# Experts' tiles written out, q and k parts in halves, maxima spread by ScalarE, last sums in PSUM

## The chip, the core and the metric

The kernel runs on one core of one Trainium2 chip. The metric is the device time of one execution in microseconds (us): the median of three runs. Below, PE is TensorE, DVE is VectorE, ACT is ScalarE, POOL is GpSimd, and SP is SyncE, which here only starts transfers.

## The reference

Two layers on x of 16 batches of 256 rows of 128 numbers. Layer 0 is attention with a mask in 16 heads of 64, and then 16 experts of which each row uses four. Layer 1 is attention in 16 heads of 8, and then a recurrence over the batches. Each of the four parts is added to x and normalized. The last two, which most of the change touches:

```python
q = _split_heads(_lora_linear(x, Wq, Aq, Bq), b, n)   # k and v likewise
attn = jnp.einsum('bhnd,bhmd->bhnm', q, k) * SCALE
attn = jax.nn.softmax(attn, axis=-1)
out = jnp.einsum('bhnm,bhmd->bhnd', attn, v)
...
def step(c, xt):
    ft = jax.nn.sigmoid(xt @ wf.T + c @ uf.T + bf)
    it = jax.nn.sigmoid(xt @ wi.T + c @ ui.T + bi)
    gt = jnp.tanh(xt @ wc.T + c @ uc.T + bc)
    c = ft * c + it * gt
    return (c, None)
c_final, _ = lax.scan(step, c0, x)
h = jnp.tanh(jnp.einsum('tbi,oi->tbo', x, wo) + c_final @ uo.T + bo)
```

Every output needs the state after the last batch, so the final tanh of all batches comes behind the whole scan.

## The kernel before

The program has one stream of instructions on each engine, tied together by semaphores. The stages follow one another: attention of layer 0; experts; a hand-over; attention of layer 1 together with the recurrence; a last stage.

*Experts.* 4096 rows by four experts are sorted into 144 tiles of 128 rows, written to memory (xs), and gathered by tile. `tiles` computes TURN = 24 tiles: transposed rows (xgT), eight products with the first weights (line 869), gelu on ACT, eight with the second weights (878). `batch_loop` (line 42) writes two turns out, then runs a hardware loop over the turns between, then writes one out. With six turns the loop body runs three times, so each engine jumps back twice: between tiles 71 and 72, and between tiles 95 and 96.

*Hand-over.* POOL gathers each batch's expert rows (yk, line 615, four gathers in a half, two halves a batch), ACT weighs them with the gates (1146), POOL combines them (641 to 645). The deviation and norm of a batch go from DVE to POOL (rstd, a power, 623) and back. The order on POOL is `outputs(b)`: deviations, new state, first half of a fetch, keep, combine, second half.

*Layer 1.* A batch takes eight steps p of two heads each. PE makes each product of q and k twice: `scores` gives the row maxima for the next batch, and line 897 gives the transposed scores of this batch with the maxima subtracted (the maxima are three more rows of the stacked operand qst). ACT takes exponentials (1096), PE multiplies with v (909). q and k are split in three bfloat16 parts (`parts`, on ACT and DVE), stored to memory (qkd) and loaded back stacked (qst, kst) for the batch after next. SP starts all of that in order: the spread of the second half of the maxima for this batch (TMB), two stores, nine loads and one fill with zeros for the batch after next, the spread of the first half of the next batch's maxima (TMA, line 460). Line 897 waits for the first half at p = 0 and for the second at p = 4, and at each p for the exponentials of the step before. The scores of p = 0 wait for all loads of the next batch (`stk`). At p = 4 and 6 PE makes the gates of the recurrence for batch b - 2 (988, 989, 992), ACT applies sigmoid and tanh, POOL makes the new state c2 (651 to 657).

*Last stage.* After the last state PE makes the product with uo (999), DVE adds the bias to it (1480, tile `state`) and adds that to three of four groups of four batches (1484), POOL adds it to the fourth (678). ACT takes tanh of each group (1161), DVE (1491) and POOL (682) add x, the last norm follows (DVE, POOL, ACT 1166), and SP stores each group.

## Time and profile before

| what | us |
|---|---|
| median of three runs | 1545.09 (1543.08 to 1546.7) |
| profiled execution, its own time | 1541.06 |
| its span | 1539.3 |
| experts, roughly | 709 to 1001 of the span |
| hand-over | 1001 to 1079 |
| batches of layer 1 | 1079 to 1464 |
| last stage | 1464 to 1539.3 |

The prediction is for the median; rows of the trace belong to the profiled execution. Over the span PE is busy 1277.0 us (83%), DVE 1012.2, ACT 943.3 and POOL 795.4. Such shares hide that the stages differ, so the views are read by stretch.

### The profile page before, as it was taken

To read this page: it belongs to the slowest core of one execution; us is meant where nothing else is said; L and a number is where in the kernel's file an instruction comes from. 1 tells how busy PE (TensorE), PEld (TensorE's weight loads), DVE (VectorE), ACT (ScalarE), POOL (GpSimd) and SP (SyncE) were. 2 spreads that over 40 slices of the span, in tenths; PEclk is the share of its full clock that TensorE was granted. 3 is DMA by queue.
4 is the path that set the end of the run, shared out by engine and by line. 5 is a ranking of instruction groups with operands and counts; after the bars stand their busy time and mean duration, and the time that the engine had idled before them with its cause. 6 is when DMAs were issued, how large, how long until landed. Compare 5 with 4: busy or idle time off the path is not lost.

```text
span 1539.3 us, 36468 instructions
## 1 busy us (share of the span) xinstructions
PE 1277.0 (83%) x9486; PEld 963.4 (63%) x9486; DVE 1012.2 (66%) x3750; ACT 943.3 (61%) x2844; POOL 795.4 (52%) x1025
## 2 busy tenths in 40 slices
PE   7999999999999999856999899903778777787870
PEld 3766666766666666636999889901445555555540
DVE  1677777777777777755777666615677677667725
ACT  5877777777777777733566556511555566555544
POOL 1557777777777777743332100166456665653133
PEclk9999999999999999977999999955899989999995
DMA  9522222222222222111222222215343434343201
GB/s 345 168 61 68 68 66 66 68 68 68 68 68 68 68 68 68 44 45 51 71 70 70 61 62 69 63 34 100 80 88 69 89 66 92 72 87 58 47 4 55
DMA packets 150447, 115.49 MB, mean 75 GB/s; under 512 B 11809, under 2 KB 139937, under 8 KB 148290
## 3 DMA queue, kind: packets, MB, share of 16 engines
q1 hardware_dynamic: 142146, 97.50, 24.7%
q0 software_dynamic: 8192, 16.79, 4.0%
q8 instruction: 38, 0.62, 0.2%
q14 instruction: 71, 0.58, 0.1%
HBM read 50.02 MB, written 61.08 MB: 72 GB/s over the span
## 4 chain that ended last, share of the span: by engine, by line
PE 28%; DMA 7%; issue 5%; DVE 5%; DVEq 3%; POOL 2%; ACT 2%; another core or an unknown queue 2%; SPq 1%; POOLq 1%; ACTq 0%
PE psum L869 9%; PE psum L878 8%; DMA qst<-mrow 3%; PE psum L909 3%; DMA wall<-mrow 3%; PE psum L897 2%; PE psum L972 2%; POOL yk L615 1%; PE psum L855 1%; PE psum L988 1%; ACT wall L1096 1%; DVE mx L1396 1%; PE psum L989 1%; DMA yk<-ys,posc 1%
## 5 line engine op out<-in xcount | busy, mean ns | idle before, releaser
L526 POOL TENSOR_SCALAR P<-P,rinv 128x192 f32<-128x192 f32 (+1 forms) x384 | 308.5, 817 | 163.9 <-DVE rinv L1223 161.2
L1056 ACT ACTIVATE P<-shifted,least 128x192 f32<-128x192 f32 (+1 forms) x512 | 240.3, 471 | 113.0 <-DVE least L1209 112.3
L1086 ACT ACTIVATE hid<-psum,wA 128x128 f32<-128x128 f32 x576 | 164.4, 368 | 118.3 <-PE psum L869 118.2
L1396 DVE TENSOR_REDUCE mx<-psum 128x2 f32<-128x512 f32 x256 | 165.6, 687 | 78.4 <-PE psum L972 54.1
L1096 ACT ACTIVATE wall<-psum 128x1024 f32<-128x1024 f32 x128 | 130.9, 1022 | 93.8 <-PE psum L897 73.7
L1209 DVE CUSTOM_DVE_ANT_0 shifted<-psum,band 128x192 f32<-128x192 f32 (+1 forms) x512 | 168.7, 384 | 27.6 <-PE psum L747 27.3
L869 PE MATMUL psum<-xgT,wA 128*128 128x128 f32 x1152 | 156.7, 280 | 7.6 <-DVE xgT L1362 7.6
L516 POOL DMA_INDIRECT xs<-x1c,pos x128 | 127.9, 999 | 57.9 <-issue 29.6
L615 POOL DMA_INDIRECT yk<-ys,posc x128 | 124.7, 974 | 55.7 <-issue 29.3
L878 PE MATMUL psum<-wB,hid 128*128 128x128 f32 x1152 | 153.3, 277 | 0.0
L869 PEld LDWEIGHTS psum<-xgT,wA 128*128 128x128 f32 x1152 | 144.1, 197 | 8.3 <-issue 8.3
L878 PEld LDWEIGHTS psum<-wB,hid 128*128 128x128 f32 x1152 | 141.5, 194 | 0.0
L783 PEld LDWEIGHTS psum<-ident,P 128*128 128x128 f32 x1024 | 117.5, 141 | 36.3 <-issue 29.3
L783 PE MATMUL psum<-ident,P 128*128 128x128 f32 x1024 | 134.9, 275 | 3.6 <-POOL P L526 1.4
L747 PE MATMUL psum<-kT,qT 64*128 64x192 f32 (+1 forms) x1024 | 131.5, 375 | 0.6 <-DVE least L1209 0.6
L801 PE MATMUL psum<-PT,V 128*64 128x256 f32 (+1 forms) x1024 | 111.0, 359 | 0.7 <-DVE PT L1197 0.7
L747 PEld LDWEIGHTS psum<-kT,qT 64*128 64x128 f32 x1024 | 80.2, 186 | 38.6 <-issue 37.4
L1355 DVE COPY wA<-wall 128x516 f32 x144 | 61.9, 430 | 60.6 <-ACT hid L1086 39.8
L1056 ACT ACTIVATION_READ_ACCUMULATOR P<-shifted,least 128x1 f32 x512 | 95.8, 187 | 0.0
L698 PE MATMUL psum<-hT,wg 128*128 (+1 forms) x256 | 88.9, 429 | 1.8 <-ACT kT L1013 0.9
L1197 DVE COPY PT<-psum 128x448 f32<-128x448 f32 x128 | 79.0, 617 | 17.3 <-PE psum L801 8.5
L801 PEld LDWEIGHTS psum<-PT,V 128*64 128x64 f32 x1024 | 67.9, 136 | 30.2 <-issue 8.1
(243 smaller groups left out, 2547.5 us busy)
## 6 DMA issues: line engine op xcount, KB each, us to landing
xs<-zrow SPq DMA_DIRECT2D x33, 1024.0 KB
xg<-xs SPq DMA_DIRECT2D x144, 64.0 KB, 1.8
ys<-yrow SPq DMA_DIRECT2D x72, 128.0 KB, 1.8
wall<-in_wall SPq DMA_DIRECT2D x1, 8232.0 KB, 35.9
qkd<-parts SPq DMA_DIRECT2D x32, 192.0 KB
qst<-qkd SPq DMA_DIRECT2D x66, 64.0 KB
wall<-qkd SPq DMA_DIRECT2D x35, 64.0 KB
kst<-qkd SPq DMA_DIRECT2D x11, 192.0 KB
```

Of the source, the lines that this page charges most:

```text
L526: g.tensor_scalar(x, x, rinv[:, par, n:n + 1], None, ALU.mult).then_inc(s["pn_ready"], 1)
L615: g.indirect_dma_start(out=yk[:, slot, count * half + n, :], out_offset=None, in_=ys, in_offset=bass.IndirectOffsetOnAxis(posc[:, half, n: ...
L747: last = mm(bk[:, c0:c0 + w], qT[64 * h:64 * h + 64, p, it * 128:(it + 1) * 128], kT[64 * h:64 * h + 64, p, 0:w], start=True, stop=True)
L783: last = nc.tensor.transpose(bk[:, c0:c0 + 128], P[:, par1, it, h, jt * 128:(jt + 1) * 128], ident[:, :])
L801: last = mm(OTB[64 * h:64 * h + 64, k * N + c0:k * N + N], V[:, jt, r * 128 + 64 * h:r * 128 + 64 * h + 64], PT[:, k, h, keys], start=(jt ...
L869: mm(UP[two][:, at:at + GT], wA[:, p % 4, f * 128:(f + 1) * 128], xgT[:, p % 4, :], start=True, stop=True).then_inc(s["up_mm"], 1)
L878: last = mm(DN[two][:, 0:D], hid[:, m, f, :], wB[:, m, f * D:(f + 1) * D], start=(f == 0), stop=(f == FC - 1))
L1056: last = sc.activation(P[:, par, it, h, 0:w], shifted[:, par, it, h, 0:w], ACT.Exp, scale=-1.0, bias=least[:, par, n:n + 1], accum_out=row ...
L1086: sc.activation(hid[:, p % 4, f, :], UP[two][:, at:at + GT], ACT.Gelu, bias=wA[:, p % 4, F + f:F + f + 1]).then_inc(s["hid_ready"], 1)
L1096: sc.activation(pc[:, p % 4, :, :, :].rearrange("q h j n -> q (h j n)"), ST, ACT.Exp, scale=SCALE1).then_inc(s["exps1"], 1)
L1209: v.tensor_tensor_reduce(out=shifted[:, par, it, h, 0:w], in0=bk[:, c0:c0 + w], in1=band[:, it, 0:w], scale=-SCALE0, scalar=3.0e38, op0=AL ...
L1396: v.tensor_reduce(out=mx[:, :, h], in_=SB[(par + 1 + h) % 3].rearrange("q (i n) -> q i n", i=TT), axis=mybir.AxisListType.X, op=ALU.max).t ...
```

## The change

1. All 144 experts' tiles are written out on SP, PE, ACT and DVE; no loop is left there (TURN is 8, which sets only how many one call writes).
2. qkd holds q and k by halves of the heads. Four stores of 64 partitions take the place of two of 128; each load is as large as before, in twice as many pieces of half the size. The matrix cwqk is put in the same order, in four DVE operations for two.
3. The maxima are spread by a transfer that ACT starts right after its own copy, no longer by SP.
4. In step 7 PE makes the scores ahead of the transposes of x2 and x3.
5. POOL's first gathers are interleaved with combine and deviations, and ACT weighs the rows of two early batches at another place.
6. POOL adds the bias bo2 to each batch's output xo; the last two states are made on DVE.
7. In the last stage the sums are made in PSUM: PE brings the outputs in with the identity (`outputs_in`, eight matmuls of 128x512) and adds the state's product (`state_in`, sixteen matmuls of 256 columns). ACT's tanh reads PSUM. The tile `state`, DVE's lines 1480 and 1484 and POOL's 678 and 682 go. Of the last group ACT scales half and DVE half, and it is stored in two parts.

```diff
-TURN = 24
+TURN = 8
...
-        qkd = nc.dram_tensor("qkd", (2, NPART, 128, N), bf16, kind="Internal").ap()
+        qkd = nc.dram_tensor("qkd", (2, 2, NPART, 64, N), bf16, kind="Internal").ap()
...
-            batch_loop(sp, 2, NT // TURN - 1, 2, body)
+            for i in range(NT // TURN + 1):
+                body(i)
...
             def attention(b, par):
-                if has(b, 0):
-                    spread_maxima(b, TMB, par, 1)
                 if has(b, 2):
                     load = (par + 2) % 3
                     need_alone(sp, "parts_ready", b + 3)
                     need_alone(sp, "stk", 16 * NSTK * (b + 2))
                     for w in range(2):
-                        sp.dma_start(qkd[w].rearrange("a r n -> r a n"), parts[:, :, w * N:(w + 1) * N]).then_inc(s["qkd_out"], 16)
-                    need_alone(sp, "qkd_out", 32 * (b + 3))
+                        for e in range(2):
+                            sp.dma_start(qkd[w, e].rearrange("a r n -> r a n"), parts[64 * e:64 * e + 64, :, w * N:(w + 1) * N]).then_inc(s["qkd_out"], 16)
+                    need_alone(sp, "qkd_out", 64 * (b + 3))
                     need_alone(sp, "st_full", 8 * b)
-                    rows = qkd.rearrange("w a (d h) n -> w (a d) h n", h=H1)
+                    rows = [qkd[w].rearrange("e a (d h) n -> (a d) e (h n)", h=H1 // 2) for w in range(2)]
+                    q, k = [x[load].rearrange("q (e h) n -> q e (h n)", e=2) for x in (qst, kst)]
                     n = 0
                     for qa in range(NPART):
                         count = NPART - qa
-                        sp.dma_start(kst[load][DH1 * n:DH1 * (n + count), :, :], rows[1, 0:DH1 * count, :, :]).then_inc(s["stk"], 16)
-                        for k in range(count):
-                            sp.dma_start(qst[load][DH1 * (n + k):DH1 * (n + k + 1), :, :], rows[0, DH1 * qa:DH1 * (qa + 1), :, :]).then_inc(s["stk"], 16)
+                        sp.dma_start(k[DH1 * n:DH1 * (n + count), :, :], rows[1][0:DH1 * count, :, :]).then_inc(s["stk"], 16)
+                        for m in range(count):
+                            sp.dma_start(q[DH1 * (n + m):DH1 * (n + m + 1), :, :], rows[0][DH1 * qa:DH1 * (qa + 1), :, :]).then_inc(s["stk"], 16)
                         n += count
-                    sp.dma_start(qst[load][MROW:MROW + NMAX, :, :], no_maxima).then_inc(s["stk"], 16)
-                if has(b, 1):
-                    spread_maxima(b, TMA, (par + 1) % 3, 0)
...
+            sp.wait_ge(s["fin_ready"], GROUPS)
+            store(8 * GROUPS - 8, 4)
+            sp.wait_ge(s["fin_dve"], 1)
+            store(8 * GROUPS - 4, 4)
...
+                if has(b, -2):
+                    need_alone(pool, f"free{GB[0]}", tally[GB[0]].before(b, GB[1] + 1))
+                    xo = xo_all[:, bass.ds((b - 2) * TT, TT), :]
+                    g.tensor_tensor(xo, xo, bo2[:, :].rearrange("q (o d) -> q o d", o=1).to_broadcast([128, TT, D]), ALU.add).then_inc(s["xo_kept"], 1)
...
-            for b in range(-5, 2):
+            fetch(-5, -5 % 3, 0)
+            fetch(-5, -5 % 3, 1)
+            fetch(-4, -4 % 3, 0, 0, 2)
+            combine(-4, -4 % 3)
+            fetch(-4, -4 % 3, 0, 2, 3)
+            deviations(-3)
+            fetch(-4, -4 % 3, 0, 3, 4)
+            fetch(-4, -4 % 3, 1)
+            keep(-3)
+            fetch(-3, -3 % 3, 0)
+            combine(-3, -3 % 3)
+            fetch(-3, -3 % 3, 1, 0, 1)
+            deviations(-2)
+            fetch(-3, -3 % 3, 1, 1, 4)
+            keep(-2)
+            fetch(-2, -2 % 3, 0)
+            combine(-2, -2 % 3)
+            fetch(-2, -2 % 3, 1)
+            for b in range(-1, 2):
...
-            xo, xt = group(GROUPS - 1)
-            pool.wait_ge(s["state_ready"], 1)
-            g.tensor_tensor(xo, xo, per_batch(state), ALU.add).then_inc(s["h_pre_last"], 1)
.then_inc(s["last_sum"], 1)
...
+                        if isinstance(b, int) and b == B + 1:
+                            last_gates(b)
+                        else:
+                            need(pe, "scan_done", b - 1)
+                            need_x2T_x3T(pe, b)
+                            gates(b, GA)
+                    if p == 5 and isinstance(b, int) and b == B:
+                        outputs_in(0)
+                        outputs_in(1)
...
+                    scores(b, p, nxt)
                     if p == 7 and (has(b, 3) or has(b, -1)):
...
-                    scores(b, p, nxt)
...
+            def last_gates(b):
+                need_x2T_x3T(pe, b)
+                parts = (GA, 0, 0), (GA, 1, 1), (GB, 0, 2)
+                for use, n, k in parts:
+                    need_free(pe, b, use)
+                    mm(shared(use)[:, n * N:(n + 1) * N], gw[:, k, :], x3T[:, :], start=(n == 0), stop=False)
+                for it in range(TT):
+                    mm(shared(GB)[:, N + it * D:N + (it + 1) * D], x3T[:, it * 128:(it + 1) * 128], gw[:, 3, :], start=False, stop=False)
+                outputs_in(2)
+                need(pe, "scan_done", b - 1)
+                for use, n, k in parts:
+                    last = mm(shared(use)[:, n * N:(n + 1) * N], gu[:, k, :], c2[:, :], start=False, stop=(n == 1 or use == GB))
+                    if n == 1 or use == GB:
+                        last.then_inc(s[f"full{use[0]}"], 1)
+            def outputs_in(c):
+                need(pe, "xo_kept", 4 * (c + 1))
...
+                for half in range(2):
+                    mm(bank[2 * c + half][:, :], ident[:, :], xo_all[:, 8 * c + 4 * half:8 * c + 4 * half + 4, :].rearrange("q t d -> q (t d)"), start=True, stop=False)
+            def state_in(c):
+                wo3 = gu[:, 3, :].rearrange("q (o d) -> q o d", o=1).to_broadcast([128, 2, D])
+                for half in range(2):
+                    for it in range(TT):
+                        last = mm(bank[2 * c + half].rearrange("q (k i d) -> q k i d", k=2, i=TT)[:, :, it, :], c2[:, it * 128:(it + 1) * 128], wo3, start=False, stop=(it == TT - 1))
+                last.then_inc(s["h_full"], 1)
             attention_loop(pe, attention)
             pe.wait_ge(s["scan_done"], B + 1)
-            for it in range(TT):
-                last = mm(SB[0][:, it * D:(it + 1) * D], c2[:, it * 128:(it + 1) * 128], gu[:, 3, :], start=True, stop=True)
-            last.then_inc(s["state_mm"], 1)
+            state_in(0)
+            state_in(1)
+            outputs_in(3)
+            state_in(2)
+            state_in(3)
...
+                    if p == 1 and isinstance(b, int) and b in (-2, -1):
+                        for half in range(2):
+                            weigh(b - 1, (b - 1) % 3, half)
...
-            def maxima_row(b, use, half):
+            def maxima_row(b, use, slot, half):
                 need_full(act, b, use)
                 sc.activation(mrow[:, half, :], shared(use).bitcast(bf16)[0:NMAX, 0:N], ACT.Copy).then_inc(s[f"free{use[0]}"], 1)
+                need_alone(act, f"free{use[0]}", tally[use[0]].before(b, use[1] + 1))
+                hh = H1 // 2
+                act.dma_start(qst[slot][MROW:MROW + NMAX, half * hh:half * hh + hh, :],
+                              mrow[:, half, :].rearrange("q (o n) -> q o n", o=1).to_broadcast([NMAX, hh, N])).then_inc(s["mrow_in"], 16)
...
+                act.wait_ge(s["h_full"], c + 1)
+                sc.activation(xo_all[:, 8 * c:8 * c + 8, :].rearrange("q t d -> q (t d)"), psum[:, 1024 * c:1024 * c + 1024], ACT.Tanh).then_inc(s["h_act"], 1)
...
+                    if p == 7 and isinstance(b, int) and b >= B:
+                        dve.wait_ge(s["gate_act"], b - 1)
+                        v.scalar_tensor_tensor(tf[:, :], tf[:, :], 1.0, c2[:, :], ALU.add, ALU.mult)
+                        v.scalar_tensor_tensor(tg[:, :], ti[:, :], 1.0, tg[:, :], ALU.add, ALU.mult)
+                        v.drain()
+                        v.scalar_tensor_tensor(c2[:, :], tf[:, :], 0.5, tg[:, :], ALU.mult, ALU.add).then_inc(s["scan_done"], 1)
...
-            dve.wait_ge(s["state_mm"], 1)
-            need(dve, f"free{GB[0]}", tally[GB[0]].before(B + 2))
-            v.tensor_tensor(state[:, :, :], SB[0][:, 0:N].rearrange("q (i d) -> q i d", i=TT), bo2[:, :].rearrange("q (o d) -> q o d", o=1).to_broadcast([128, TT, D]), ALU.add)
-            v.drain().then_inc(s["state_ready"], 1)
-            for c in range(GROUPS - 1):
-                xo, xt = group(c)
-                v.tensor_tensor(xo, xo, per_batch(state), ALU.add).then_inc(s["h_pre"], 1)
             def squared(c):
                 x, h = x_all[:, 8 * c:8 * c + 8, :], xo_all[:, 8 * c:8 * c + 8, :]
+                dve.wait_ge(s["h_act"], c + 1)
+                v.tensor_tensor(x, x, h, ALU.add)
...
+                if c == GROUPS - 1:
+                    for k in range(4, 8):
+                        x = x_all[:, 8 * c + k, :]
+                        last = v.tensor_scalar(x, x, mv2[:, c, k, 0:1], rstd2[:, c, k:k + 1], ALU.subtract, ALU.mult)
+                    last.then_inc(s["fin_dve"], 1)
```

SP in a batch of layer 1, before: the stores of the parts, the loads for the batch after next (tile wall is one of three that hold qst and kst), then the spread of the maxima.

```order
L440 DMA qkd<-parts 128x3x256 x2
L448 DMA wall<-qkd 24x4096
L450 DMA wall<-qkd 8x4096 x3
L448 DMA wall<-qkd 16x4096
L450 DMA wall<-qkd 8x4096 x2
L448 DMA wall<-qkd 8x4096
L450 DMA wall<-qkd 8x4096
L452 DMA wall<-zeros 24x4096
L460 DMA qst<-mrow 24x8x256 x2
```

The same place now.

```order
L432 DMA qkd<-parts 64x3x256 x4
L441 DMA wall<-qkd 24x2x2048
L443 DMA wall<-qkd 8x2x2048 x3
L441 DMA wall<-qkd 16x2x2048
L443 DMA wall<-qkd 8x2x2048 x2
L441 DMA wall<-qkd 8x2x2048
L443 DMA wall<-qkd 8x2x2048
L445 DMA wall<-zeros 24x2x2048
L432 DMA qkd<-parts 64x3x256 x4
```

The last row before is gone from SP; the stores are four, the pieces 2x2048 for 4096.

ACT in a batch before: an exponential, the copy of the maxima, weighing of gathered rows, exponentials and copies between.

```order
L1096 ACTIVATE wall<-psum 128x1024
L1151 ACTIVATE mrow<-psum 24x256
L1146 ACTIVATE yk<-yk,gcur 128x128 x4
L1096 ACTIVATE wall<-psum 128x1024
L1100 ACTIVATE oTc<-psum 128x256
L1146 ACTIVATE yk<-yk,gcur 128x128 x4
L1096 ACTIVATE wall<-psum 128x1024
```

The same place now.

```order
L1155 ACTIVATE wall<-psum 128x1024
L1211 ACTIVATE mrow<-psum 24x256
L1214 DMA qst<-mrow 24x8x256
L1205 ACTIVATE yk<-yk,gcur 128x128 x4
L1155 ACTIVATE wall<-psum 128x1024
L1159 ACTIVATE oTc<-psum 128x256
L1205 ACTIVATE yk<-yk,gcur 128x128 x4
L1155 ACTIVATE wall<-psum 128x1024
```

The spread of the maxima stands between ACT's copy and its next work.

PE at the program's end, before: the last gates, then the product of state and uo.

```order
L989 MATMUL psum<-c,gu 128x256
L988 MATMUL psum<-x3T,gw 128x256
L989 MATMUL psum<-c,gu 128x256
L992 MATMUL psum<-gw,x3T 128x128 x2
L999 MATMUL psum<-gu,c 128x128 x2
```

The same place now: products of x3T, outputs (wall, with the identity), then those that need the state c.

```order
L1017 MATMUL psum<-x3T,gw 128x256 x3
L1019 MATMUL psum<-gw,x3T 128x128 x2
L1041 MATMUL psum<-wall,ident 128x512 x2
L1023 MATMUL psum<-c,gu 128x256 x3
L1048 MATMUL psum<-gu,c 128x2x128 x8
L1041 MATMUL psum<-wall,ident 128x512 x2
L1048 MATMUL psum<-gu,c 128x2x128 x8
```

What doesn't need the last state moved ahead of it, and the sums of the groups came in.

## Rows read from the trace of the kernel before

**Rows 1.** Busy time by stretch: length, busy us per engine, granted clock, DMA share, GB/s.

```profile
756.00:804.00 48.00, 48.00 (x433) 48.00 (x432) 35.59 (x103) 28.55 (x101) 16.05 (x27) 1.00 0.25 72
1001.00:1079.00 78.00, 16.02 (x53) 7.48 (x54) 24.75 (x63) 13.98 (x41) 50.44 (x66) 0.52 0.33 67
1079.00:1464.00 385.00, 305.78 (x2544) 203.40 (x2544) 276.72 (x822) 223.81 (x441) 198.79 (x268) 0.93 0.38 74
1464.00:1539.30 75.30, 27.11 (x194) 18.54 (x192) 33.23 (x143) 33.62 (x68) 26.89 (x29) 0.71 0.11 30
```

**Rows 2.** Timeline of PE over a back edge: start, duration, instruction, idle and releaser.

```profile
850.81 1.07 PE L869 MATMUL psum<-xgT,wA 128*128 128x128 f32 x8
...
856.75 2.01 PE L869 MATMUL psum<-xgT,wA 128*128 128x128 f32 x8 [3.87 <-DVE xgT L1362]
...
860.38 1.06 PE L869 MATMUL psum<-xgT,wA 128*128 128x128 f32 x8
```

**Rows 3.** Waits over the second back edge: total us, times, longest us.

```profile
DVE wA L1355 <- issue: 4.3, 3, 3.4
...
PE psum L869 <- DVE xgT L1362: 3.8, 1, 3.8
```

**Rows 4.** Timeline of the hand-over.

```profile
1029.24 0.16 DVE L94 TENSOR_TENSOR u<-rstd 128x2 f32<-128x2 f32 x1 [5.25 <-POOL rstd L623]
...
1054.67 1.28 ACT L1146 ACTIVATE yk<-yk,gcur 128x128 f32<-128x128 f32 x4 [16.77 <-DMA yk<-ys,posc]
...
1066.23 0.37 ACT L1151 ACTIVATE mrow<-psum 24x256 bf16<-24x256 bf16 x1 [3.71 <-issue]
...
1078.95 1.03 PE L897 MATMUL psum<-qst,kst 128*128 128x256 bf16 x4 [6.86 <-DMA qst<-mrow]
```

**Rows 5.** Chain that ended last: start, duration, step.

```profile
1044.32 10.33 DMA yk<-ys,posc
...
1069.37 9.54 DMA qst<-mrow
...
1087.65 2.43 DMA qkd<-parts
...
1531.81 3.85 ACT x_all L1166 x10
```

**Rows 6.** Line 460, the spread of the maxima: its issues, and who waited for it.

```profile
L460 SPq DMA_DIRECT2D qst<-mrow x22: 778/818/1583, 1069.4 to 1468.2; - x22
...
  PE psum L897: 34.9, 11
```

**Rows 7.** Timeline of three places in the batches of layer 1.

```profile
1101.03 1.02 ACT L1096 ACTIVATE wall<-psum 128x1024 f32<-128x1024 f32 x1 [1.35 <-remote]
...
1102.64 1.03 PE L897 MATMUL psum<-qst,kst 128*128 128x256 bf16 x4 [2.97 <-DMA qst<-mrow]
...
1103.60 1.94 PE L909 MATMUL psum<-wall,v 128*32 128x256 f32 x16
...
1387.03 0.60 PE L897 MATMUL psum<-wall 128*128 128x256 bf16 x4
...
1387.99 1.07 PE L909 MATMUL psum<-wall,v 128*32 128x256 f32 x16 [0.36 <-DVEq L1462]
...
1438.98 1.02 ACT L1096 ACTIVATE wall<-psum 128x1024 f32<-128x1024 f32 x1
...
1444.16 1.04 PE L897 MATMUL psum<-wall 128*128 128x256 bf16 x4 [4.34 <-DMA wall<-mrow]
```

**Rows 8.** Waits in the batches: total us, times, longest us.

```profile
POOL rstd L623 <- DVE ve L89: 108.3, 16, 16.4
```

**Rows 9.** Timeline after the last gates.

```profile
1500.38 0.40 POOL L651 TENSOR_SCALAR tf<-tf 128x256 f32<-128x256 f32 x1 [6.15 <-ACT tg L1122]
...
1504.07 1.22 PE L999 MATMUL psum<-gu,c 128*128 128x128 f32 x4 [4.39 <-POOL c L657]
1505.32 0.42 DVE L1480 TENSOR_TENSOR state<-psum,bo 128x256 f32<-128x256 f32 x1 [15.18 <-PE psum L999]
...
1509.31 4.27 ACT L1161 ACTIVATE wall<-wall 128x1024 f32<-128x1024 f32 x4 [8.85 <-DVE wall L1484]
1511.47 1.21 DVE L1491 TENSOR_TENSOR x_all<-x_all,wall 128x1024 f32<-128x1024 f32 x1
```

**Rows 10.** Groups by line: instructions, busy us, mean ns, idle before.

```profile
L705 PE MATMUL psum<-wg,hV 128*128 128x512 f32 x128 | 66.6, 602 | 3.3 <-issue 1.7 <-DVE V L1184 0.8 <-DVE rconst L1179 0.4
...
L615 POOL DMA_INDIRECT yk<-ys,posc x128 | 124.7, 974 | 55.7 <-issue 29.3 <-POOL posc L612 26.4
```

More of the change, by code:

```diff
@@ L647, in new_state @@
             def new_state(b):
-                if has(b, -2):
+                if has(b, -2) and not (isinstance(b, int) and b >= B):
                     need_alone(pool, "gate_act", b - 1)
@@ L879, in tiles @@
                         last.then_inc(s["dn_mm"], 1)
-            batch_loop(pe, 2, NT // TURN - 1, 2, tiles)
+            for i in range(NT // TURN + 1):
+                tiles(i)
             pe.wait_ge(s["c_set"], 1)
@@ L912, in attention @@
                     if p == 4 and has(b, -2):
-                        need(pe, "scan_done", b - 1)
-                        need_x2T_x3T(pe, b)
-                        gates(b, GA)
-                    if p == 6 and has(b, -2):
+                        if isinstance(b, int) and b == B + 1:
[7 more added lines that the diff above has]
+                        outputs_in(1)
+                    if p == 6 and has(b, -2) and not (isinstance(b, int) and b == B + 1):
                         gates(b, GB)
@@ new lines, in outputs_in @@
+            def outputs_in(c):
+                need(pe, "xo_kept", 4 * (c + 1))
+                if c == 0:
+                    need(pe, "exps1", 8 * B)
+                if c in (1, 2):
+                    need(pe, "max_done", H1 * B)
+                if c == 2:
+                    need(pe, "o_free", 4 * B)
+                    need(pe, "to_free", 4 * B)
+                if c == 3:
+                    for k in range(2):
+                        need(pe, f"free{k}", tally[k].before(B + 2))
+                for half in range(2):
+                    mm(bank[2 * c + half][:, :], ident[:, :], xo_all[:, 8 * c + 4 * half:8 * c + 4 * half + 4, :].rearrange("q t d -> q (t d)"), start=True, stop=False)
@@ L1135, in attention @@
                         last.then_inc(s[f"free{TX[0]}"], 1)
-                    if p == 7 and isinstance(b, int) and b == -3:
-                        for half in range(2):
-                            weigh(b, par, half)
             def weigh(b, par, half):
@@ L1386, in tiles @@
                         weights_B(e, q)
-            batch_loop(dve, 2, NT // TURN - 1, 2, tiles)
+            for i in range(NT // TURN + 1):
+                tiles(i)
             def row_maxima(b, p, par):
```

77 lines of the change are left out of this document (31 added, 46 removed).

## Prediction

> **What bounds the kernel now.** I read the stretches first, because a share over the whole span mixes stages with different limits [rows 1]. In the experts' stretch PE is busy for the whole of its 48 us: TensorE is the bound there, and a gain can only come from places where it stops. In the hand-over (1001 to 1079) PE works 16.02 of 78 us and POOL 50.44: the limit is a chain over POOL, transfers and short steps. In the batches of layer 1 PE works 305.78 of 385 us, ACT 223.81, DVE 276.72, POOL 198.79: PE is the fullest engine, but 79 us of it are waits. In the last stage nothing is above half; a serial chain runs through it.
>
> Then I looked for the waits that end last in each stage. In the loop of the experts PE starts a tile's eight matmuls at 850.81, the next at 856.75 and the next at 860.38 [rows 2]; where PE is full the distance is 1.89 (48 us hold 433 matmuls [rows 1], 17 to a tile). The wait of 3.87 is on DVE's copy of the transposed rows; The second way back to the loop's start repeats it with 3.8, and DVE's own idle there, up to 3.4, is put down to issue: it waited for no engine, only for the jump [rows 3].
>
> In the hand-over ACT has batch 0's maxima ready at 1066.23 + 0.37 = 1066.60, but the transfer that spreads them is issued at 1069.37, after the loads on SP, and takes 9.54; PE starts batch 0's first products of layer 1 at 1078.95, after 6.86 idle [rows 4, 5]. Earlier there, DVE waits 5.25 for POOL's rstd, which stands behind gathers of 0.97 each [rows 4, 10].
>
> In the batches that same transfer is what line 897 waits for, 11 times, 34.9 us in all, the hand-over's 6.86 among them [rows 6]. Not all of this is to be won: the first products also need the last exponentials of the batch before. At 1102.64 these ended at 1101.03 + 1.02 = 1102.05, so 0.59 hangs on the transfer alone; at 1444.16 they ended at 1440.00, so 4.16 does [rows 7]. Worked out likewise for all 14 starts from 1102.64 to 1444.16 it sums to 16.6 us.
>
> In the tail POOL makes the last state from 1500.38 on, PE starts at 1504.07, DVE makes the state tile at 1505.32 and adds it to the groups, so ACT's first tanh is at 1509.31 after 8.85 idle and DVE's first sum at 1511.47 [rows 9].
>
> **The change part by part.** All sums are against the profiled execution: its span is 1539.3, its own time 1541.06, which is 4.0 below the median 1545.09; the 4 are added at the end.
>
> *Tiles written out.* Both ways back go. At the first the two distances are 856.75 - 850.81 = 5.94 and 860.38 - 856.75 = 3.63; less twice 1.89 that is 5.8. The second, from its wait of 3.8, gives 5.6. Sum -11.4. Tiles 0 to 47 were written out before, and the stretch with PE full, 756 to 804, lies in the second half of them [rows 1], so straight code of this kind costs nothing that I can see there. Bounds -10.5 to -12.
>
> *Hand-over.* The issue moves to ACT's queue, right behind the copy: up to 2.77 (1069.37 - 1066.60) earlier, and no loads ahead of it on that queue. Alone, the transfer is nearest to a store of q and k parts at 2.43 [rows 5]; at worst it keeps its 9.54. PE's own idle is 6.86, and no more than that comes from this step. POOL's new order takes each rstd between two gathers: of the 5.25 I take 3 (a gather or two of 0.97 still stand ahead, and POOL's total work stays). Moving ACT's weighing takes x2T out from behind a wait of 16.77 for gathered rows [rows 4]; I price it within the 3. Sum -10; bounds -6 (2.77 and 3, the transfer no faster) and -12 (6.86 and 5.25).
>
> *Maxima from ACT in the batches.* At most 16.6 is to be won by the transfer. What is late next is the loads of the following batch: the transfer stood behind them on one queue, so they end at most its own 2.4 before it, and the scores of step 0 need them some 1.7 us (0.60 and 1.07 of products) after the first products start. Starts with over about 2 to win, such as the 4.16, therefore keep a part: -13. PE's clock: the stage runs at 0.93 granted [rows 1], and line 909's sixteen took 1.94 right behind the wait at 1102.64 and 1.07 elsewhere [rows 7], the two levels 1.2 and 2.4 GHz; line 897's four likewise 1.03 and 0.60. That is 1.3 us a start, and by the same two lines I counted 10 starts at the lower level, those with about 2 us or more of idle PE ahead. With the idle cut, I count 6: -8; bounds 0 and -13. Scores ahead of the transposes at step 7 give ACT its next exponentials up to one pair of transposes (0.4 to 0.9) earlier and make x2T that much later: -0.2 a batch, -3; bounds 0 and -7.5.
>
> The costs. ACT now issues two transfers a batch. SP's issues took 0.78 to 1.58, median 0.82 [rows 6], and behind them on ACT stand exponentials for which PE's next products wait. ACT is busy 58% of the stage, so most of it falls in its idle time; with cover gone it would be 1.6 a batch. I take 0.3, so +5 in 16 batches; bounds 0 and +6.5. POOL's extra addition costs about 0.73 as its others of that size (1500.38 to 1504.07 holds five), and is covered by 108.3 us of waits for DVE, 6.8 a batch [rows 8]: +2, for the share that falls ahead of an rstd; bounds 0 and +5. Four stores for two: SP waits there for other engines, two more issues of 0.82 stand ahead of loads that are late next, of which I take +1; bounds 0 and +3. Sum -13 - 8 - 3 + 5 + 2 + 1 = **-16**; bounds -37 and, with the gains 0, +14.
>
> *Tail.* Four 128x512 matmuls stand ahead of the gates GB at batch step 16. Line 705's 128x512 cost 0.52 a record, two records to a matmul [rows 10], so 1.04 and 4.2 together. In return the state moves from POOL (1500.38 to 1504.07, 3.7) to DVE, where three operations cost some 0.42 each as line 1480's [rows 9], 1.3 to 1.5, twice. The x3T products of the last gates go ahead of the wait. After the last state PE needs four products for group 0 in PSUM (2 to 3.5), ACT one tanh of 1.07 (4.27 for four). So DVE's first sum starts near 1503.6 for 1511.47: -7.9. DVE then makes four sums of 1.21 where POOL made the last: +1.2. ACT's last eight scales, in a run of 3.85 for ten [rows 5], are shared with DVE: -1.5, and I keep +0.7 for PE pacing the later groups. Sum -7.5; bounds -3 (PE at its lower level, 0.71 granted in this stretch [rows 1]) and -11.
>
> Sum: -11.4 - 10 - 16 - 7.5 = -44.9. 1541.06 - 44.9 = 1496.2, and with the 4.0 of the median **1500**.
>
> **The rivals.**
> *Another queue does not help.* The transfer would share its engines with the loads and land when it did. For it: a gather on POOL's own queue took 10.33 beside loads [rows 5]. Against it: the store that had nothing ahead on its queue took 2.43 [rows 5], and the maxima's place behind the loads explains 9.54 by itself. Then the stage gives -3 for the order of scores and +8 of costs, the hand-over -6: -11.4 - 6 + 5 - 7.5 = -20, so 1525. The Trainium skill ("DMA: Bandwidth & Descriptors", section "Issuing engines are not separate DMA queues") states this rule: transfers interleave on the same 16 engines whoever starts them, and a second issuer saves only the time to initiate. By that rule 1525 is the time; the trace agrees with the 10.33, and the 2.43 of a store does not decide it.
>
> *More is won.* All 16.6, the clock at every start (13), the scores' order in full (7.5), costs 3: -34 for the stage; hand-over -12, tail -11, loop -11.4. That is -68: 1477. Against it: the loads that are late next.
>
> *Slower.* ACT's issues stand wholly on the path, with no gain in the batches. 32 issues at the longest, 1.58, are +50.6; against the -29 of loop, hand-over and tail that is +22: 1567. It decides at 29/32 = 0.9 an issue; the median 0.82 is just below. For it: exponentials stand right behind each issue. Against: ACT's 42% idle, and the issue time is the queue's own, not shown to stop the engine.
>
> *Nothing comes of it* where that same price is near 0.9: gains and costs meet at 1545.
>
> **How the numbers follow.** Forecast 1500 (own range 1488 to 1512) 0.56; another queue does not help, 1525, 0.20; more is won 0.14; slower 0.06; no change 0.04. Differences within 0.2%, 3 us, can't be told from none here. So faster 0.90, same 0.04, slower 0.06. The range reaches to both neighbours: 1475, where the stage's lower bound would nearly be met, to 1526.
>
> **What would show it.** Loop: tile starts 1.89 apart throughout, and the experts' stretch 11 shorter. Hand-over: line 897's products of batch 0 at about 1078.95 - 11.4 - 10 = 1057.5, without a wait on the maxima. Batches: the spread landing in 3 to 6 us, the wait of line 897 on it below 10 in all, loads or exponentials named in its place, and L909's sixteen at 1.07 in most starts. Tail: DVE's first sum about 8 us sooner after the start of batch 14 than before (1511.47 - 1444.16 = 67.3). Wrong would be: the spread still landing after 8 us or more (another queue does not help), ACT idle vanishing and PE waiting for exponentials by over 1.8 a batch more (slower), or the stretch of the experts no shorter.

## The result and the profile after

The changed kernel took 1535.9 us in the median of 15 runs (1524.55 to 1540.86), the kernel before 1546.7 in 15 runs timed beside it (1541.29 to 1551.83). The ratio is 0.9922, with a 95% interval of 0.9903 to 0.9941: 0.8% faster, where 3% had been forecast (1500 for 1545). The profiled execution of the changed kernel has a span of 1531.4, 7.9 less than before.

I split that span by the starts of the experts' tiles and of ACT's exponentials. Before and after: first to last tile 284.4 and 272.6; from the last tile to the first exponential of layer 1 84.4 and 81.4; from there to the first exponential of the last batch 385.1 and 397.4; from there to the end 74.2 and 69.7. So the loop gave 11.8, the hand-over 3.0, the tail 4.5, and the batches lost 12.3. The remaining 1.0 lies ahead of the experts.

Busy time by stretch of the changed kernel, in the columns of [rows 1]; the stretches are the same parts of the program, with their new limits:

```profile
756.00:804.00 48.00, 48.00 (x432) 48.00 (x432) 35.78 (x102) 28.97 (x102) 15.60 (x27) 1.00 0.25 72
989.00:1058.00 69.00, 14.45 (x54) 7.15 (x55) 21.23 (x58) 11.37 (x35) 46.88 (x60) 0.52 0.36 70
1058.00:1461.00 403.00, 316.09 (x2544) 206.68 (x2542) 278.47 (x830) 222.27 (x448) 214.43 (x285) 0.89 0.39 72
1461.00:1531.40 70.40, 39.42 (x236) 26.16 (x236) 31.48 (x147) 31.47 (x63) 18.43 (x20) 0.85 0.11 32
```

The batches are the third row: longer than before, at a lower granted clock (0.89 for 0.93). In the groups by line of the changed kernel the wait of the loop's two jumps is gone: line 878 now is line 869 of before, and nothing is left of the 7.6 us of idle PE that it had over all tiles.

```profile
L878 PE MATMUL psum<-xgT,wA 128*128 128x128 f32 x1152 | 154.5, 278 | 0.0
```

The spread of the maxima, in the changed kernel's view of its line (answers to [rows 6]) and in its chain that ended last (answers to [rows 5]):

```profile
L1214 ACTq DMA_DIRECT2D qst<-mrow x22: 803/804/1482, 1047.8 to 1465.2; - x22
...
  PE psum L907: 23.3, 10
```

```profile
1053.19 7.77 DMA yk<-ys,posc
...
1078.99 8.83 DMA qst<-mrow
...
1103.67 9.51 DMA wall<-mrow
...
1186.49 10.59 DMA wall<-mrow
```

ACT starts it now, and it lands no sooner: 8.8 to 10.6 us after its issue in these rows of the chain, where [rows 5] had 9.54. The prediction had named over 8 us as a sign that it was wrong. PE still waits for it 10 times, 23.3 us in all. The timeline of a batch's start (answers to [rows 7]) reads as before, with the sixteen products with v (line 919, 909 before) at the lower clock, 1.94 where 1.07 is the full one:

```profile
1087.87 1.04 PE L907 MATMUL psum<-qst,kst 128*128 128x256 bf16 x4 [3.25 <-DMA qst<-mrow]
...
1088.84 1.94 PE L919 MATMUL psum<-wall,v 128*32 128x256 f32 x16
```

The hand-over in the changed kernel's timeline (answers to [rows 4]):

```profile
1047.33 0.37 ACT L1211 ACTIVATE mrow<-psum 24x256 bf16<-24x256 bf16 x1 [4.69 <-PE psum L996]
...
1047.81 1.48 ACTq L1214 DMA_DIRECT2D qst<-mrow  x1
...
1057.78 1.06 PE L907 MATMUL psum<-qst,kst 128*128 128x256 bf16 x4
...
1061.37 1.28 ACT L1205 ACTIVATE yk<-yk,gcur 128x128 f32<-128x128 f32 x4 [10.69 <-DMA yk<-ys,posc]
...
1064.22 1.02 ACT L1155 ACTIVATE wall<-psum 128x1024 f32<-128x1024 f32 x1
1065.30 1.04 PE L907 MATMUL psum<-qst,kst 128*128 128x256 bf16 x4 [3.48 <-ACT wall L1155]
```

PE's first products start at 1057.78, as forecast (1057.5), without a wait. But ACT's first exponentials stand behind weighing, which waits until 1061.37 for gathered rows (in the chain above, 7.77 from 1053.19). PE's second step is at 1065.30: 7.5 after the first, where it was 2.15 before (1078.95 to 1081.10).

One batch, on SP and ACT (the loads that follow the first are left out):

```profile
1317.78 2.18 SPq L432 DMA_DIRECT2D qkd<-parts  x4
...
1322.06 0.30 SPq L441 DMA_DIRECT2D wall<-qkd  x1
...
1325.23 0.80 ACTq L1214 DMA_DIRECT2D qst<-mrow  x1
...
1326.21 1.28 ACT L1205 ACTIVATE yk<-yk,gcur 128x128 f32<-128x128 f32 x4 [1.09 <-issue]
```

From the stores' start to the first load, which needs all four to have landed, 4.28 us pass. ACT stands still for 1.09 around its issue, and for 1.0 to 1.7 around each of its 32 issues in this trace: the issue is not free for the engine.

The tail (answers to [rows 9]):

```profile
1486.94 3.60 PE L1041 MATMUL psum<-wall,ident 128*128 128x512 f32 x8
...
1492.39 0.42 DVE L1541 SCALAR_TENSOR_TENSOR tf<-tf,c 128x256 f32<-128x256 f32 x1 [4.51 <-ACT tg L1184]
...
1501.13 3.72 PE L1048 MATMUL psum<-gu,c 128*128 128x256 f32 x16 [2.52 <-DVE c L1544]
...
1504.29 1.23 DVE L1552 TENSOR_TENSOR x_all<-x_all,wall 128x1024 f32<-128x1024 f32 x1 [3.21 <-ACT wall L1222]
```

### The profile page after: what moved, and what is told of

The parts are those of the page before. It is cut to its first block, busy times and chain, and to the rows that moved or that the text cites. A ratio compares the mean times of both kernels' runs of the same rounds, so it can differ in the third digit from the quotient of the medians.

```text
span 1531.4 us, 35991 instructions
## 1 busy us (share of the span) xinstructions
PE 1294.2 (85%) x9530; PEld 969.9 (63%) x9530; DVE 1014.0 (66%) x3758; ACT 936.9 (61%) x2840; POOL 799.4 (52%) x1029
## 4 chain that ended last, share of the span: by engine, by line
PE 28%; DMA 7%; issue 4%; ACT 4%; DVE 3%; another core or an unknown queue 3%; POOL 3%; DVEq 1%; POOLq 1%; SPq 0%; ACTq 0%
PE psum L878 9%; PE psum L887 8%; DMA qst<-mrow 4%; PE psum L919 3%; PE psum L907 2%; DMA wall<-mrow 2%; ACT wall L1155 2%; POOL yk L608 2%; PE psum L988 2%; PE psum L864 1%; DVE mx L1460 1%; PE psum L1004 1%; DMA qst<-zeros 1%; DVE st L83 1%
## 5 line engine op out<-in xcount | busy, mean ns | idle before, releaser
L1460 DVE TENSOR_REDUCE mx<-psum 128x2 f32<-128x512 f32 x256 | 164.9, 686 | 84.4 <-PE psum L988 49.1
```

The lines of the kernel that those rows point to most:

```text
L1460: v.tensor_reduce(out=mx[:, :, h], in_=SB[(par + 1 + h) % 3].rearrange("q (i n) -> q i n", i=TT), axis=mybir.AxisListType.X, op=ALU.max).t ...
```

## The experiments

Two theories stood at first. **Theory 1**: the batches lose what ACT's issue of the spread takes from ACT. **Theory 2**: stores, loads and spread are one chain of transfers that sets the length of a batch; the stores in halves make it longer, and the spread lands when the loads have, whoever starts it. Two more are about single parts. **Theory 3**: the new order of step 7 makes x2T, and with it the q and k parts, late. **Theory 4**: the hand-over's gain is given back because the first exponential stands behind weighing. All ratios are to the kernel before, timed beside each run (1546.7 us beside the changed kernel, 1540.4 to 1541.3 beside the others).

For each profiled execution I worked out two lengths in ten batches from the middle (medians): from the first store's issue to the completion of the last store, and to that of the last load. "Batches" is the time from the first exponential of batch 1 to that of batch 15. It comes from one execution each, and it varies: two pairs of kernels below that have the same batches differ in it by 4.3 (357.2 and 361.5, whole parts and weighing later) and 8.5 (336.6 and 345.1, q in one load and the products moved at the end). So the ratios decide, and a difference of a few us in this column doesn't.

| kernel | ratio (95%) | stores end, us | loads end, us | batches, us |
|---|---|---|---|---|
| before | 1 | 2.50 | 15.7 | 361.4 |
| changed | 0.9922 (0.9903 to 0.9941) | 3.96 | 18.0 | 372.7 |
| changed, spread on SP | 1.0004 (0.9988 to 1.002) | 4.06 | 17.3 | 377.9 |
| changed, whole parts | 0.9858 (0.9836 to 0.9879) | 2.57 | 16.0 | 357.2 |
| changed, scores last | 0.9908 (0.9883 to 0.9933) | 4.11 | 17.5 | 369.2 |
| before, loop alone | 0.9885 (0.986 to 0.9909) | 2.53 | 16.2 | 360.7 |
| before, halves alone | 1.0183 (1.0166 to 1.02) | 4.35 | 17.9 | 378.7 |
| before, four stores | 1.0133 (1.0097 to 1.0168) | 4.32 | 17.5 | 380.1 |
| before, spread on ACT | 0.9988 (0.997 to 1.0007) | 2.58 | 15.7 | 362.7 |
| before, zeros first | 0.9887 (0.9853 to 0.9922) | 2.80 | 14.2 | 356.9 |

**Spread on SP again.**

```diff
-                act.dma_start(qst[slot][MROW:MROW + NMAX, half * hh:half * hh + hh, :],
+                sp.dma_start(qst[slot][MROW:MROW + NMAX, half * hh:half * hh + hh, :],
```

(in `spread_maxima` on SP, at its place of before.)

> The changed kernel with the spread of the maxima started by SP again, behind the loads; all else as changed. Theory 1 (ACT stops for each issue, and the spread lands behind the loads whoever starts it): the steps 1 and 5 get back about 0.3 and 1.1 us each, so the batches of layer 1 are 12 to 18 us shorter than changed, and the time is about 1520 to 1524, ratio to before 0.983 to 0.986; the spread lands 8 to 11 us after its issue as it does now. Theory 2 (the four stores make the loads late, the issue on ACT is covered): no gain, or a loss of up to 5 us, ratio 0.991 to 0.995.

By the ratios it was 0.8% slower than the changed kernel (1.0004 and 0.9922), not faster: theory 1 falls as the main cause. Theory 2 had expected a loss of at most 5 us; this is about 13. So the spread on ACT is worth something beside stores in halves. In the two profiled executions 5.2 us of it lie in the batches and 3.2 between batch 0's first exponential and batch 1's.

**Whole parts.**

```diff
-                        for e in range(2):
-                            sp.dma_start(qkd[w, e].rearrange("a r n -> r a n"), parts[64 * e:64 * e + 64, :, w * N:(w + 1) * N]).then_inc(s["qkd_out"], 16)
+                        sp.dma_start(qkd[w].rearrange("a r n -> r a n"), parts[:, :, w * N:(w + 1) * N]).then_inc(s["qkd_out"], 16)
```

> The changed kernel with q and k stored and loaded whole again (two stores of 128 partitions, pieces of 8 KB); the spread stays with ACT. Theory 2 (the stores in halves end 1.4 us later, and with them the loads and the spread): the batches are 10 to 20 us shorter than changed, ratio to before 0.980 to 0.986. Theory 1 (ACT's issue is the loss): within 4 us of changed, ratio 0.990 to 0.995.

The ratio is 0.0064 lower, 10 us, and the intervals don't meet: theory 2. The batches of this execution are 15.5 shorter than in the changed kernel, and 4.2 shorter than before. SP's timeline of this kernel, a batch:

```profile
1284.28 0.55 SPq L431 DMA_DIRECT2D qkd<-parts  x2
1287.21 0.06 SPq L440 DMA_DIRECT2D kst<-qkd  x1
```

First load 2.93 after the stores' start, where it was 4.28; the loads take as long (12.7 for 13.3).

**Scores last.**

```diff
-                    scores(b, p, nxt)
                     if p == 7 and (has(b, 3) or has(b, -1)):
...
+                    scores(b, p, nxt)
```

> The changed kernel with the scores of step 7 behind the transposes again. If the order of step 7 makes x2T and with it the q and k parts late (theory 3), the batches are 5 to 10 us shorter than changed, ratio 0.986 to 0.989. Theories 1 and 2 expect nothing or a loss of up to 5 us: ratio 0.991 to 0.996.

The interval overlaps that of the changed kernel: whether the order alone does anything is not shown here.

**The loop alone.**

```diff
-            batch_loop(pe, 2, NT // TURN - 1, 2, tiles)
+            for i in range(NT // TURN + 1):
+                tiles(i)
```

> The kernel before with nothing but the experts' tiles written out. The gaps at the two jumps go: 11.4 us less, time near 1535, ratio 0.9925, and the rest of the span as before. If written-out tiles cost something in the rest (code that is fetched), the gain is under 8 us, ratio over 0.995.

First to last tile takes 272.9 for 284.4: 11.5 less, as forecast, and batches, hand-over and tail are within 1.5 of before. The time fell by 1.15%, 17.7 us; the rest of this, 5 to 7 us, lies ahead of the experts in the profiled execution (first tile at 704.7 for 711.2). That start varies from 704.7 to 711.5 over the profiled executions of all kernels here, one of each; why stays open. The loop alone gives at least as much as the whole change (0.9922): the other parts together brought nothing beyond it that the ratios show.

**Halves alone, and four stores alone.** In the second the layout and the loads are those of before:

```diff
-                        sp.dma_start(qkd[w].rearrange("a r n -> r a n"), parts[:, :, w * N:(w + 1) * N]).then_inc(s["qkd_out"], 16)
+                        for e in range(2):
+                            sp.dma_start(qkd[w, :, 64 * e:64 * e + 64].rearrange("a r n -> r a n"), parts[64 * e:64 * e + 64, :, w * N:(w + 1) * N]).then_inc(s["qkd_out"], 16)
```

> The kernel before with nothing but the q and k parts stored and loaded by halves of the heads. Theory 2 (stores, loads and the spread behind them are one chain of transfers that sets the batch's length; four stores make it some 2 us longer): the batches of layer 1 are 12 to 20 us longer, time ratio 1.008 to 1.013, the stores end 4.0 after their start where it was 2.5. Theory 1 (the issue on ACT is the loss, not the stores): within 0.2% of before.

> The kernel before with four stores of 64 partitions instead of two of 128, the layout in memory and the loads unchanged (pieces of 8 KB). If the stores' number is what the halves cost, the stores end 1.5 to 1.9 us later and nearly all of the 28 us of the halves alone come back: ratio 1.012 to 1.018. If the loads' pieces of 4 KB are the cost, ratio 1.000 to 1.004.

The halves alone cost 1.83%, 28 us, more than expected. In the chain that ended last of that kernel, store and spread follow each other in batch after batch, as [rows 5] showed once:

```profile
1092.53 3.35 DMA qkd<-parts
...
1099.69 9.46 DMA qst<-mrow
...
1120.92 2.27 DMA qkd<-parts
...
1126.99 9.73 DMA wall<-mrow
```

The four stores alone do it with the loads untouched (380.1 and 378.7). SP's timeline of the four stores:

```profile
1342.29 2.46 SPq L441 DMA_DIRECT2D qkd<-parts  x4
1346.85 0.33 SPq L449 DMA_DIRECT2D wall<-qkd  x1
```

So most of it is the stores' number and not the loads' smaller pieces; whether the layout adds something (1.0183 and 1.0133) is not told apart, since the intervals just meet. From the first issue to the end of the last, four take 2.6 us and two 0.8 (medians of ten batches, here and in the kernel before), for the same bytes.

**The spread on ACT alone, in the kernel before.** The edit is part 3 of the change.

> The kernel before with nothing but the spread of the maxima started by ACT. Theory 2: the spread still lands 0.5 to 0.8 us behind the end of the loads, so the batches gain little; what SP's own waits and issues had added in the hand-over goes (up to 3 us), ratio 0.994 to 1.000. The prediction's step (own queue, lands in 3 to 6 us, clock back) would give 0.986 to 0.990. Theory 1 (ACT stops at each issue) gives 1.005 to 1.012.

Within 0.3% of before: the step that I had priced highest is worth nothing that can be measured by itself. Theory 1 falls here once more: the exponentials of step 6 start 3.5 us after those of step 5, where it was 2.3 before (medians), so ACT's stop is there, and it costs no time that can be measured.

**Zeros first**, in the changed kernel with whole parts and in the kernel before.

```diff
+                    need_alone(sp, "st_full", 8 * b)
+                    sp.dma_start(qst[load][MROW:MROW + NMAX, :, :], no_maxima).then_inc(s["stk"], 16)
                     need_alone(sp, "parts_ready", b + 3)
...
-                    sp.dma_start(q[MROW:MROW + NMAX, :, :], no_maxima).then_inc(s["stk"], 16)
```

> The changed kernel with whole parts, and the fill with zeros (24 x 8 KB) issued ahead of the stores, while SP waits for the parts, where it was the last of the ten loads. Theory 2: about 2 us less stand between the stores and the landing of the spread in each batch, the batches are 15 to 30 us shorter than with whole parts alone, ratio 0.967 to 0.976. If the loads are not what the batches wait for, ratio 0.985 to 0.988 as with whole parts alone.

> The kernel before with nothing but the fill with zeros ahead of the stores. Theory 2 for the kernel before (stores, loads, spread are the chain that sets the batch's length there too): 1 to 2 us less a batch, 15 to 30 us, ratio 0.981 to 0.990. If the kernel before was bound by PE with the spread only now and then late, as the prediction had it (16.6 us at most), ratio 0.991 to 1.000.

Measured 0.9748 (0.9725 to 0.977) and 0.9887 (0.9853 to 0.9922). The same work, moved out of the chain, gives 1.1% of both kernels (0.9858 to 0.9748, and 1 to 0.9887). In the profiled execution of the second the loads ended 1.5 sooner in a batch (14.2 for 15.7), but the batches are only 4.5 shorter (that execution was the slowest of its six, 1532.0 with a median of 1526.2); in the first they are 13.6 shorter (343.6 for 357.2). So the chain was on the path in the kernel before too. Other waits stood close behind it there: in seven of 15 starts of the second the spread's last packet had ended 2.5 us or more ahead of PE's first products, and in none before.

**q in one load.** q is stored with its copies, in three stores for one, and loaded as 48 rows.

```diff
+                        sp.dma_start(qd[n:n + count].rearrange("a r n -> r a n"), parts[:, qa:qa + 1, 0:N].to_broadcast([128, count, N])).then_inc(s["qkd_out"], 16)
...
+                    sp.dma_start(qst[load][0:DH1 * len(PRODUCTS), :, :], qrows).then_inc(s["stk"], 16)
```

> As the run with the zeros first, and q is stored with its copies, so that it is one load of 48 rows instead of six of 8. The same bytes are loaded, spread over 16 engines and not over 8, and the stores move 384 KB instead of 192 for q. Theory 2: loads end some 3 us sooner, less 1 to 1.5 for the stores; 10 to 30 us less than with the zeros first alone, ratio 0.950 to 0.967, until PE's own work (about 21 us a batch) is the bound. If the landing is set by bytes or by something other than the engines that the loads use, no gain or a loss.

0.9697 (0.9671 to 0.9723), 8 us less than with the zeros first alone: the direction of theory 2, less than its 10 to 30. The spread's line in this kernel names PE's products as a waiter no longer, only three weight loads, and the clock of its batches is 0.97:

```profile
L1215 ACTq DMA_DIRECT2D qst<-mrow x22: 803/804/1424, 1044.2 to 1418.7; - x22
...
  PEld psum L908: 4.8, 3
```

```profile
1054.60:1414.60 360.00, 293.01 (x2546) 198.43 (x2545) 281.31 (x830) 223.18 (x446) 213.25 (x285) 0.97 0.41 87
```

**Weighing later in the hand-over** (with whole parts).

```diff
                     if p == 1 and has(b, 0):
...
+                    if p == 1 and isinstance(b, int) and b == 0:
+                        weigh(-1, -1 % 3, 1)
```

> The changed kernel with whole parts, and ACT weighs the second half of the rows of the last batch ahead of layer 1 behind the first exponentials of batch 0 instead of ahead of them. Theory 4 (the hand-over's gain is given back because the first exponential stands behind weighing, which waits for POOL's gathers): the stretch from batch 0's start to batch 1's is 4 to 6 us shorter than 29.4, ratio 0.981 to 0.984. If something else holds the first exponentials (the loads of batch 1, x2T), nothing changes, ratio 0.985 to 0.988.

The first exponential came 4.6 sooner after the last tile (80.1 for 84.7), as theory 4 says, yet the ratio stayed 0.9858 (0.9839 to 0.9878): from there to batch 15 it took 6.0 longer. What held the first exponential was found; that it is worth anything to move it was not shown.

**Four more on the run with q in one load.** The spread on SP; the first four products with the identity behind the gates GB; with that, scores last; and then spread on SP and scores last together, with the products at their place.

> The run with q in one load, and the spread started by SP again. There the spread no longer ends the wait of the batch's first products (1.3 us in all beyond the exponentials). Theory 2 with ACT's stop of about 1.1 us at step 5 and 0.3 at step 1: with the transfers off the path ACT's issue is what is left, so SP is better by 5 to 15 us, ratio 0.960 to 0.966. If the queue matters still (SP puts the spread behind the loads again), equal or slower: ratio 0.969 to 0.976.

> The run with q in one load, and the first four products with the identity at the end stand behind the gates GB of batch step 16 instead of ahead of them, under the making of the state. If their 3.4 us lie on the chain of the last two states, as the trace of the changed kernel has it, the end comes 2 to 4 us sooner, ratio 0.966 to 0.968; if they only fill PE's idle time there, no change, 0.969 to 0.971.

> As the run before, and the scores of step 7 behind the transposes again. With the transfers off the path, PE, ACT and DVE bound the batches. If the scores' order gives ACT its exponentials sooner, this is 3 to 7 us slower, ratio 0.969 to 0.973; if it makes the parts late, 3 to 7 us faster, ratio 0.961 to 0.965; within 2 us the order is worth nothing here.

> The changed kernel with q in one load, the zeros first, the spread started by SP and the scores of step 7 behind the transposes. The parts that helped or did no harm, together: ratio 0.962 to 0.967. If either of the last two needs the other's absence, 0.968 to 0.972.

Measured: 0.9668 (0.9639 to 0.9698), 0.972 (0.9697 to 0.9742), 0.967 (0.9648 to 0.9691), 0.9658 (0.9628 to 0.9689). The last is the fastest, 1488.2 beside 1540.4, and beats both kernels clearly; against q in one load with ACT and the scores first (0.9697) it is not told apart. The moved products shortened the tail by 2.2, but the batches of that execution, which the edit leaves alone, took 345.1 for 336.6, and the ratio shows no gain: the expectation's second reading. Scores last was better than scores first by 0.5% in one pair (0.967 and 0.972), while the changed kernel's pair showed nothing that can be told apart.

## Why the prediction was wrong

**The loop: right.** -11.4 was forecast, -11.8 and, alone, -11.5 came.

**The batches: wrong, and this decides.** The step was "The issue moves to ACT's queue, right behind the copy", with "no loads ahead of it on that queue", so that the spread would land as if alone, "nearest to a store of q and k parts at 2.43"; from it came "-13" and "-8". Its time when alone was right; that another queue lets it run alone was not. The trace of the changed kernel holds both cases. The second half of the maxima goes out when SP has no loads under way, and all 16 of these transfers landed 2.4 to 2.9 us after their issue. The first half, for which a batch's first products wait, goes out beside the loads, and 14 of these 16 landed after 8.3 to 11.0 (the last, with no loads left, after 2.6). In the kernel before, on SP's queue, the medians are about 2.5 and 9. What line 907 waits for the spread beyond the exponentials, worked out as the 16.6, is 16.8 now: nothing of it was won. The rival "Another queue does not help" had the mechanism, though its 1525 was too low as well, for the stores. What the chip did can be seen in the packets of one first-half spread of the changed kernel, issued at 1298.10 and landed at 1307.07 (transfers of three windows; q10 is ACT's queue, q1 SP's, q0 POOL's; packets, MB, share of 16 engines):

```profile
q1 hardware_dynamic: 98, 0.29, 62.1%
q0 software_dynamic: 24, 0.06, 11.9%
q10 hardware_dynamic: 68, 0.03, 7.7%
...
q1 hardware_dynamic: 84, 0.25, 48.5%
q0 software_dynamic: 41, 0.07, 7.0%
...
q0 software_dynamic: 64, 0.13, 25.3%
q10 hardware_dynamic: 136, 0.07, 15.0%
q1 hardware_dynamic: 15, 0.03, 5.4%
```

The windows are 1298.1 to 1301.1, 1301.1 to 1304.9 and 1304.9 to 1307.1. A third of the spread's 204 packets went at once, none in the 3.8 us in which SP's loads were still at work, and two thirds when those were all but over. The second-half spread ahead of it, issued at 1284.83, has the transfers of its window (1284.8 to 1287.5) to itself:

```profile
q10 hardware_dynamic: 204, 0.10, 16.5%
```

So in the median of ten batches the first half landed 0.4 to 0.7 behind the last load in every kernel of the table, on either queue; in single batches of the changed kernel it came up to 3.4 ahead of it. The Trainium skill ("DMA: Bandwidth & Descriptors", section "Issuing engines are not separate DMA queues") has the rule that I set against the step and then gave 0.20: transfers use the same 16 engines whoever starts them. The runs agree: the spread on ACT alone gave 0.9988. That they interleave, as the same section of the Trainium skill says, the windows above do not show for this pair of queues: there the spread stood still for 3.8 us, and the measurement decides.

**The clock.** The "-8" was to come from the starts. Of the 14 starts ten were at the lower level before and seven in the changed kernel, so some of it came there, and yet the clock of the stage fell from 0.93 to 0.89: it was lost inside the batches. The prediction put the lower level at the starts "with about 2 us or more of idle PE ahead"; the rows don't quite say that, since one of the ten had 0.74 ahead and a start with 2.08 ran at the full level.

**The stores: the term that was mis-sized most.** I took "+1" for two more stores and called SP's time a wait for others. Alone they cost 28 us with the layout, 20 us (0.0133 of 1540) without it, and in the changed kernel 10. The mistake is behind both steps: I read the loads and the spread as two waits of which the spread was the later one, and asked what it hung on beyond the exponentials (16.6 us). In the kernel before a batch's stores start some 10 us after its first products, and from there to the landing of the spread, which the next first products wait for, it took 16.2; the period is 26.6. That the two fill it says by itself only that PE starts when the spread lands; that they set it was shown by the runs that made the chain longer or shorter (four stores 1.0133, zeros first 0.9887). A wait that looks short on PE can be the end of a chain as long as the batch, because all that PE does ahead of it is paced by the batch before.

**ACT's issue.** Priced at 0.3 a batch, on the ground that it was "not shown to stop the engine". It does: the trace shows the idle of 1.1 at step 5, and the exponentials of step 6 came 1.3 later, on the mean of nine batches of layer 1 (4.17 for 2.88 from step 5). But no run shows that this costs time: 0.9988 alone in the kernel before, and 0.9668 against 0.9697 with the spread back on SP in the run with q in one load, where the intervals overlap.

**The hand-over.** -10 was forecast; -3.0 came up to the first exponential. PE's first products came "without a wait on the maxima" and close to the forecast (1057.78 for 1057.5), but partly by luck: the spread took its 9.5 as before, so its earlier issue gave 2.7 where 6.86 was taken, and the maxima were ready 6.1 sooner after the last tile, where 3 was taken. And I ended the chain at those products. What counts is the first exponential, which stands on ACT behind the weighing of rows that POOL gathers; the step had priced that weighing "within the 3" of POOL's order.

**The tail.** -7.5 was forecast, -4.5 came. Four products with the identity took 3.6 (4.2 forecast), two more 1.88; the state on DVE took 1.6 (1.3 to 1.5 forecast). Mis-sized was the "-7.9" of DVE's first sum. From batch 14's start, the prediction's own mark, it came 3.1 sooner (64.2 for 67.3), from batch 15's 3.8. The gates of step 16 stood behind the first four products, and two more lay ahead of the last gates; putting the four behind the gates made the tail 2.2 shorter in one execution, so that is part of it.

**Open.** Why halves cost 28 us in the kernel before, while undoing them in the changed one gives 10. The spread on ACT is worth 0.8% beside them and nothing measurable without them, which fits, but how the two meet on SP was not isolated. How much of the batches' change is the granted clock (0.93 to 0.89) was not tried apart, and it could be much: PE's same 2544 products are busy 316.09 us in the changed kernel's batches and 305.78 before, 10.3 more, beside the 12.3 that the batches lost. Whether the clock fell because of the later transfers or lengthened the batches by itself no run tells; with the transfers out of the way (q in one load) it was 0.97.

## What to carry to other kernels

Add up the transfers of one turn of a pipeline, from the value that they start on to the one that waits for the last of them, and compare with the period: here 10 + 16 was the whole of it, though PE looked 79% busy. Then lengthen or shorten that chain alone in a run, because the sum does not prove that it sets the pace. Here it got shorter by taking work out of it (a fill that needs no data went ahead of the stores) and by one wide load for six; a second queue did nothing, and more, smaller stores made it longer. Before counting on a transfer's time alone, look for the same transfer in the trace with and without others beside it. And follow an earlier start to the next engine before counting it.

## What the runs showed of the hardware

- Four stores of 64 partitions took 2.6 us of issue and 4.0 to 4.4 to land, two of 128 with the same bytes 0.8 and 2.5 to 2.8 (medians).
- One load of 48 rows for six of 8, with twice the bytes stored, was faster by 0.5% of the kernel, and the spread went off the path of PE's products.
- A transfer of 96 KB landed 2.4 to 2.9 us after its issue when no loads ran, and mostly 8.3 to 11.0 beside the loads of another queue. In one of these it moved no packet for 3.8 us, after a third of it had gone at once.
- ACT stood idle for 1.0 to 1.7 us around each transfer that it started.
